# Another order of the tiles in SBUF: large tiles begin at multiples of 512 bytes

## What is computed

```python
xn = layernorm(x)
# a state-space layer: 64 heads of 64 channels, 8 groups, state of 128
proj = xn @ in_proj_w.T                      # gate 4096, x 4096, B 1024, C 1024, dt 64
xBC  = silu(causal_conv(hbc, taps=4))        # x, B and C, each channel by itself
dt   = softplus(dt + dt_bias);  dA = exp(dt * -exp(A_log))
state_t = state_{t-1} * dA_t + (dt_t * x_t) (outer) B_t      # per head
y_t  = state_t . C_t + D * x_t
y    = y * rsqrt(mean(y*y over a group) + eps) * norm_weight * silu(gate)
s    = y @ out_proj_w.T
# a second branch
g    = silu(xn @ W.T + bias + lora(xn))
out  = x + s * g
```

## The kernel before

| tiles, in order | start within 512 bytes |
|---|---|
| xn_hi, xn_lo, out_sum, wconv_hi/lo, wgate_hi/lo, wout_hi/lo, stage0/1, xc0/1 | 128 |
| tails, edge, edge_in (72 bytes each, 96 with rounding) | 128, 224, 320 |
| decay0/1/2, dtx0/1, skip, xw, b_tok | 416 |
| last (32 bytes) | 416 |
| square, square_sum, sgate, cpre0/1, ynt_hi/lo, state0/1, prefix_dt, total_bc, io, x_again, eye8 | 448 |
| ones, convw_sb, convb_sb, normw_sb, dskip_sb and ten more small ones | various |

## Time and profile before

### The profile page before, as it was taken

The page is one execution under the profiler, slowest core; times in us unless marked ns, Lnnn a source line. Parts: engine busy times, 40 slices in busy tenths (PEclk is TensorE's granted clock), DMA queues, the critical chain, the costliest instruction groups (busy, mean ns, idle before and its releaser), DMA issues.

```text
span 1816.7 us, 30557 instructions
## 1 busy us (share of the span) xinstructions
PE 1769.6 (97%) x11416; PEld 1424.8 (78%) x11416; DVE 1531.0 (84%) x1945; ACT 813.7 (45%) x1803; POOL 1148.9 (63%) x1149
## 2 busy tenths in 40 slices
PE   6999999999999999999999999999999999999996
PEld 4777888888888888878777788888888888888874
DVE  6868888888888888888888988889898888888886
ACT  4554354454535344443534444454444435444442
POOL 5536658574755757475697847648474755757477
PEclk9999999999999999999999999999999999999998
DMA  7533234243323423233574333233242333423233
GB/s 234 175 134 105 105 105 139 74 136 102 108 105 105 140 89 121 105 105 115 176 227 141 118 113 127 106 102 132 80 130 103 118 105 105 140 78 109 105 116 128
DMA packets 113508, 220.77 MB, mean 122 GB/s; under 512 B 10449, under 2 KB 46673, under 8 KB 113361
## 3 DMA queue, kind: packets, MB, share of 16 engines
q1 hardware_dynamic: 112320, 218.66, 36.2%
q10 hardware_dynamic: 1040, 0.16, 0.1%
HBM read 204.63 MB, written 14.16 MB: 120 GB/s over the span
## 4 chain that ended last, share of the span: by engine, by line
PE 84%; DVE 6%; ACT 3%; issue 3%; POOL 3%; DMA 1%; SPq 0%; DVEq 0%; POOLq 0%; ACTq 0%
PE ps_conv L1156 9%; PE ps_conv L1159 9%; PE ps_conv L1162 6%; PE ps_y L1315 6%; PE ps_out L1159 6%; PE ps_out L1156 6%; PE ps_gate L1156 6%; PE ps_gate L1159 6%; PE ps_y L1320 5%; PE ps_s L1350 5%; PE ps_out L1162 5%; PE ps_gate L1162 4%; PE turned_x L1242 3%; PE ps_conv L1163 2%; DVE xc L801 2%
## 5 line engine op out<-in xcount | busy, mean ns | idle before, releaser
L801 DVE SCALAR_TENSOR_TENSOR xc<-ps_conv,convw_sb,xc 128x511 f32<-128x511 f32 (+2 forms) x576 | 430.4, 747 | 162.4 <-ACT xc L589 148.9
L1086 POOL TENSOR_TENSOR rstd_col<-mean_square,half 128x1 f32<-128x1 f32 x128 | 84.5, 660 | 543.9 <-ACT mean_square L719 543.9
L910 DVE TENSOR_TENSOR_SCAN decay<-decay,eye 128x1024 f32<-128x1024 f32 x128 | 304.1, 2376 | 0.8 <-DMA decay<-decays_d 0.8
L1104 POOL TENSOR_TENSOR cpre<-cpre,xc 128x1024 f32<-128x1024 f32 x112 | 268.5, 2397 | 0.0
L595 ACT ACTIVATE xc<-xc 128x512 f32<-128x512 f32 x192 | 120.9, 631 | 312.3 <-DVE xc L801 311.8
L1156 PE MATMUL ps_conv<-xn_hi,wconv_hi 128*128 128x512 f32 x768 | 242.9, 438 | 0.0
L1159 PE MATMUL ps_conv<-xn_hi,wconv_lo 128*128 128x512 f32 x768 | 207.9, 393 | 0.0
L1315 PE MATMUL ps_y<-decay,dtx 128*64 128x128 f32 x2048 | 197.3, 279 | 1.5 <-DVE decay L977 0.9
L1156 PEld LDWEIGHTS ps_conv<-xn_hi,wconv_hi 128*128 128x128 f32 x768 | 141.8, 195 | 49.4 <-issue 26.7
L728 ACT ACTIVATE square<-ps_y 128x512 f32<-128x512 f32 x128 | 76.8, 600 | 222.1 <-DVE ps_y L925 222.1
L1320 PE MATMUL ps_y<-cpre,state 128*64 128x128 f32 x1792 | 174.1, 273 | 0.0
(11 more groups left out here) (210 smaller groups left out, 3828.1 us busy)
## 6 DMA issues: line engine op xcount, KB each, us to landing
decay<-decays_d SPq DMA_DIRECT2D x128, 512.0 KB, 5.2
cpre<-rows_d SPq DMA_DIRECT2D x112, 512.0 KB, 3.9
stage<-w_in_t SPq DMA_DIRECT2D x32, 1024.0 KB, 6.5
stage<-w_out_t SPq DMA_DIRECT2D x16, 1024.0 KB, 5.5
stage<-w_in_t SPq DMA_DIRECT2D x32, 256.0 KB, 3.3
out_sum<-hidden SPq DMA_DIRECT2D x16, 256.0 KB, 6.1
ffn_d<-sgate SPq DMA_DIRECT2D x16, 256.0 KB, 2.3
out<-out_sum SPq DMA_DIRECT2D x16, 256.0 KB, 3.0
```

The source lines that it names most:

```text
L801: e.scalar_tensor_tensor(acc[:, d:], ps[:, 0:BLK - d], convw_sb[:, tile, TAPS - 1 - d:TAPS - d], acc[:, d:], ALU.mult, ALU.add).then_inc(S ...
L910: e.tensor_tensor_scan(d[:, :], d[:, :], eye8[:, :, :].rearrange("p h i -> p (h i)"), 0.0, ALU.mult, ALU.add).then_inc(S["scan"], 1)
L1104: e.tensor_tensor(cpre[k % 2][:, :, :], cpre[k % 2][:, :, :], xc[i // CPB % 2][:, XT + 1, block_cols(i % NCH)].unsqueeze(1).to_broadcast([ ...
```

## The change

Four small tiles (normw_sb, dskip_sb, mean_var, stats: 128, 128, 64 and 48 bytes, the last rounded to 64) move ahead of `xn_hi`. They take 384 bytes, and 16512 + 384 = 16896 = 33 x 512. The small tiles that stood between large ones (tails, edge, edge_in and last) move behind `eye8`. So every large tile from `xn_hi` to `eye8` begins at offset 0 within 512 bytes. The large tiles keep their order; they move by +384 bytes (xn_hi to xc1), +96 (decay0 to b_tok) and +64 (square to eye8). No instruction, wait, shape or order of work changes; only addresses do.

```diff
+        normw_sb = sb("normw_sb", [P, INNER // P])
+        dskip_sb = sb("dskip_sb", [P, INNER // P])
+        mean_var = sb("mean_var", [P, NCH, 2])
+        stats = sb("stats", [P, 2, 6])
         xn_hi = sb("xn_hi", [P, KT, SEQ], F32R)
         xn_lo = sb("xn_lo", [P, KT, SEQ], F32R)
         out_sum = sb("out_sum", [P, NCH, DM])
@@
         xc = [sb(f"xc{i}", [P, MT, BLK]) for i in range(2)]
-        tails = sb("tails", [P, MT, TAPS - 1])
-        edge = sb("edge", [P, MT, TAPS - 1])
-        edge_in = sb("edge_in", [P, MT, TAPS - 1])
         decay = [sb(f"decay{i}", [P, GH * P]) for i in range(3)]
         dtx = [sb(f"dtx{i}", [P, GC]) for i in range(2)]
         skip = sb("skip", [P, GC])
         xw = sb("xw", [P, GC])
         b_tok = sb("b_tok", [P, NS])
-        last = sb("last", [P, GH, 1])
         square = sb("square", [P, GC])
@@
         eye8 = sb("eye8", [P, GH, P])
+
+        tails = sb("tails", [P, MT, TAPS - 1])
+        edge = sb("edge", [P, MT, TAPS - 1])
+        edge_in = sb("edge_in", [P, MT, TAPS - 1])
+        last = sb("last", [P, GH, 1])
         ones = sb("ones", [P, 1])
         convw_sb = sb("convw_sb", [P, CONV // P, TAPS])
         convb_sb = sb("convb_sb", [P, CONV // P, 1])
-        normw_sb = sb("normw_sb", [P, INNER // P])
-        dskip_sb = sb("dskip_sb", [P, INNER // P])
@@
-        stats = sb("stats", [P, 2, 6])
-        mean_var = sb("mean_var", [P, NCH, 2])
```

## The result

The changed kernel takes 1812.8 us, the median of 17 runs, against 1816.07 us for the kernel before: the ratio is 0.9981, with a 95% interval of 0.9973 to 0.9988. It is 3.3 us faster (the interval is 2.2 to 4.9 us), where 7.8 us were forecast. Measured again beside later kernels it took 1813.3 us against 1816.4, a ratio of 0.9983 (0.9974 to 0.9992).

What follows compares the result with a forecast made beforehand. TensorE's matmul cost was taken as the bound (97% busy, 84% of the chain). Ten distances x 0.0065 us x 128 steps gave 8.3 us, 7.8 on the path: 1816.1 to 1808.3 us, own range 1805 to 1811.5, whole range 1794 to 1820.

Steps and rivals of the forecast that it cites:

- rival (a): Output product on TensorE: offsets have no effect and nothing moves, 1816.1 us with 1.5 to each side; chance 0.26.
- Bound by TensorE, other engines at 0: Whole kernel: time follows TensorE's matmul cost; VectorE, ScalarE and GpSimd gain 0, with 1 us either way for VectorE.
- DMA at 0: Transfers of decay and cpre, and first inputs: taken as 0; at most 0.8 us, and 1 us either way at the start.
- ynt is what makes the output product slow, by its place: Output product: stationary ynt at 448 costs 0.234 us a matmul, against 0.227 for the gate; it comes down to that.
- ten distances of 0.0065: Output product: ten start-to-start distances each shrink by 0.0065 us, 0.065 us a product, 8.3 us over 128 steps.
- Plain float32 at 0: Heads' matmuls on TensorE: no price seen between offsets 416 and 448, so gain 0, with 1 us to either side.
- The share on the path, 0.94: Output product: 309 of its 329 us lie on the chain, so 7.8 of the 8.3 us count.
- Rival (b): All float32r products: offset 0 is quicker than 128 too, 57 us gained, 1759 us; chance 0.13.
- Rival (c): Gate and convolution products: 128 is the good place and 0 is like 448, 20 us slower, 1836 us; chance 0.11.
- The rule of 16-byte lines: SBUF accesses: penalty depends on crossing 16-byte lines; all offsets are multiples of 16, so time stays at 1816 us.
- What would show it: Changed kernel's trace: output product's seven distances make 1.59 us, not 1.64, its mean goes from 399 towards 390 ns; gate's 1.59 stays.

Runs made afterwards that it cites:

- TensorE alone: Kernels running only the loop's matmuls, no waits or other engines, at various offsets: before and after the change differ by 26 ns a step (29 over all eight distances).
- all128: Kernel before with only tails, edge, edge_in and last moved behind eye8, so every large tile begins at offset 128: 1813.2 us against 1816.1.
- ynt128_in_before: Kernel before with unused bytes around ynt, putting it at offset 128, other large tiles at old offsets: 1811.4 us against 1816.5; again 1811.8 against 1816.4.
- ynt448_in_after: Changed kernel with unused bytes around ynt, putting it back at offset 448, everything else at 0: 1813.3 us against 1816.5.
- head_only: Kernel before with only the four small tiles moved ahead of xn_hi: 1815.9 us against 1816.1.
- ynt0_in_before: Kernel before with unused bytes around ynt, putting it at offset 0, everything else at its old offset: 1816.5 us against 1816.1.

## Why the prediction was right or wrong

The forecast was 1808.3 us; 1812.8 came. The direction and the place were right, the size was over twice too large, and the measured gain of 0.17 to 0.19% is just under the 0.2% from which I had counted "faster" (at 0.62; "same", at 0.27, is what came). 1812.8 lies outside the forecast's own range of 1805 to 1811.5 and inside the whole range only because that was drawn to hold rival (a) too.

- *Bound by TensorE, other engines at 0:* right. VectorE, ScalarE and GpSimd take the same time for the same instruction at four offsets, and TensorE alone reproduces the difference.
- *DMA at 0:* right; the 3.9 against 5.2 us was not the offset, since decay at 0 takes 5.4.
- *ynt is what makes the output product slow, by its place:* right, and all128, ynt128_in_before and ynt448_in_after show it. I left open whether the absolute offset or the distance to the partner counts; it is the distance, modulo 256.
- *The step that failed: "ten distances of 0.0065".* The sum had 65 ns a product; the median product fell by 2646 - 2627 = 19 (25 on the mean, 21 of them in the ten distances and 4 in the first). The reference I took, the gate at 0.227, follows another float32r product. The output product follows transposes in plain float32, and there nine of the changed kernel's ten distances belong to the beginning: they average 231, not 227. I had set aside only the first distance as "after plain float32", and said that the gate's was longer too; the gate of rows 8 has none such, since a convolution product runs ahead of it. The trace of before had what was needed: the convolution after a transpose, with both operands at 128, goes 314, 231, 236, 228, 233, 231 before it settles, 2606 ns in all. The right comparison was that product, not the gate, and it would still have been too kind (2646 - 2606 = 40), as the beginning isn't the same everywhere.
- *Plain float32 at 0:* wrong in its reason and wrong in size for single places. The seam from the output product to the head matmuls fell from 327 to 318 ns, the seam from gate to state update from 233 to 228, the state update's pair from 434 to 428; the convolution product behind the state update, a float32r one that the sum didn't have at all, rose by 30 in every other step. On the mean over the eight kinds of step that is -25 for the output product, -9, -5 and -5 for the others, +15 for the convolution: 28 to 29 ns a step, as the steps say. By kinds, steps without such a convolution product became 42 to 59 ns shorter, steps with it 7 to 11.
- *The share on the path, 0.94:* not tested. The steps say 28 x 128 = 3.6 us, and 3.0 to 3.3 were measured; the interval of 2.2 to 4.9 us holds both.
- *Rival (a), nothing moves:* near in size, but the distances moved. *Rival (b), 0 quicker than 128:* fell; no pair of offsets settles under 227 ns, and all at 128 and all at 0 take the same 52.504 us. The Trainium skill, page "TensorE: Matmul & The Clock Gate", section "Back-to-back issue gap", has 216 ns for 512 columns as the gap of an isolated matmul, and a shorter one for a stream; these float32r streams, at 227 ns and more, reach neither at any offset. *Rival (c), 128 the good place:* fell with all128.
- *The rule of 16-byte lines,* from the Trainium skill, page "SBUF — State Buffer", section "SBUF: two separate sides": it gave no change. What it says of crossing lines isn't contradicted: b_tok four bytes past 416 took 64 ns more in four steps than at 416, but no more than at 64 or 192, which are multiples of 16 (52.473 us all three). The rule is about one operand, and the steady distance here depends on where two lie.
- *What would show it:* I asked for 1.59 in place of 1.64 and got 1.61, with the gate unchanged. That was the right place to look.

GpSimd's small powers (rstd_col) went from 660 to 707 ns on the mean, 6 us in all; the median stayed (551 and 549), and the mean lies between 660 and 721 in the ten traces, at 684 in head_only, whose time didn't change. Why stays open; GpSimd waits 531 us ahead of them, and the steps show no trace of it. Not settled either: what in the memory makes 256 bytes the period, and what sets the length of a beginning.

## What to carry to other kernels

Where TensorE is the bound and streams float32r products, look at the distance between the starts of the stationary and the moving operand modulo 256 bytes, not at alignment of either; a small tile between large ones is enough to spoil it, and an unused piece is enough to mend it. Then measure, for a tile moved may lengthen the beginning of another product, as ynt0_in_before showed. Compare a product with one that stands behind the same kind of instruction: of twelve matmuls behind a plain float32 one, up to nine distances after the first lie above the steady rate. A few unused bytes around one tile (ynt128_in_before) beat the rearrangement of all of them, 1811.4 to 1811.8 us against 1812.8 to 1813.3.

## What the runs showed of the hardware that I had not expected

- The distance between float32r matmuls of 128 stationary and 512 moving columns at the full granted clock is 227 ns when the two operands' starts differ by a multiple of 256 bytes, 229 at 192 (stationary minus moving, modulo 256), and 232 to 234 at 32, 64, 96, 128, 160 and 224.
- After plain float32 a float32r stream at a difference of 0 has a first distance of some 312 to 319 ns behind full transposes (630 to 638 behind matmuls of 512 columns), then two to nine of some 224 to 236 ns before it settles. How many depends on where tiles lie that were read before, partners or not.
- TensorE alone, without a wait, repeats the loop's steps to a few ns: 14,753 and 12,013 ns for two kinds of step before, in the kernel and in the imitation alike.
